# Feed-forward weights of the third stage prepared beside the first and read back beside the second

## The chip, the cores and the metric

The kernel runs on 1 core of one Trainium2 chip. The metric is the device time of one execution in microseconds (us). A core has TensorE (PE; its weight loads are listed as PEld), VectorE (DVE), ScalarE (ACT), GpSimd (POOL) and SyncE (SP), which here only issues DMAs. Each works off its own queue in order, and they wait for each other by semaphores.

## The reference, cut to what matters

The input x has 32 sequences of 64 tokens with 256 features. Six blocks follow one another, each of the form `x = x + block(layernorm(x))`:

```
x = x + attention, 16 heads of 128, causal, with biases
x = x + attention over a given context (no weights)
x = x + _L0_ffn_ref(layernorm(x), ...)          # the third stage
x = x + a scan with cosines and sines of a running sum
x = x + attention over the context, 16 heads of 16
x = x + feed-forward with 4-bit weights, 2048 wide
```

The third, with h and the attention both made from its input z:

```
attn = attention16(rmsnorm(z) * ln1)            # 16 heads of 16, causal
mod  = 0.1 * tanh(attn @ A)                     # A is 256 x 16
h    = rmsnorm(z) * ln2
gate = silu(h @ W_in.T + (mod * (h @ A)) @ B)   # W_in, W_up: 1024 x 256
out  = z + (gate * (h @ W_up.T)) @ W_down.T     # W_down: 256 x 1024
```

## The kernel before

x stays in SBUF as 16 tiles of 128 tokens (`core.x`). Most matrix products are made from pairs of parts: a high part (rounded to fp32r by ScalarE) and a low part (the difference, by GpSimd or VectorE), three products for each. The program is written stage by stage; inside a stage each engine has its own block, and `run_steps` lays out a software pipeline: in step s, part number n with lag L works on unit s - L, in the order of the list. So the place in the list and the lag set an engine's order by hand.

Stage 1 (L340 to about L625) runs over 64 units, 16 heads by 4 groups of tokens; a round is 8 units, two heads. TensorE makes q and k (L440) and, for even heads, v (L422) of a unit, then transposes, scores (L455), the output product (L481) and the product with v (L472) of units further back. Each of these has one PSUM buffer, which ScalarE copies out (L506, L519, L527). The list of ScalarE ends with `split_high` and `deq.scalar`. Beside this `Dequantiser` prepares the last stage's 4-bit weights in 16 pieces: VectorE and ScalarE compute, GpSimd sums (`gpsimd_sum`) and makes the low part (`gpsimd_low`), and SP stores each to DRAM (L2216) in `later_loads`, one step of that per head: the head's weights, then `deq.store`, and in even steps `deq.load` (L2210, two loads). `deq.store` waits for `low_done`, and `gpsimd_low` of a piece stands in GpSimd's queue behind `split_low` and `gpsimd_sum` of later heads.

Stage 2 (L640 to L840) has 32 units. VectorE takes maxima (L721) and subtracts (L725) straight from PSUM.

Stage 3 begins with `token_stats`: `bn_stats` of 16 tiles (L216) unless an earlier stage has gathered them, `bn_aggr` (L219), roots. SP issues all of the stage's loads in this block (L1547 to L1550); the next block starts when every engine is through this one. Then come `split_tokens` (L280, L305), a block that prepares the small weights (among it `m_ps`, L1574), and `attention16` (L1533 on): 16 tiles in a pipeline, for this stage with `beside`, a list of functions for ScalarE and one for GpSimd. ScalarE calls them at odd tiles:

```
def weights(i, rnd, k):
    if i % 2 == 1 and i // 2 < len(beside[0]):
        beside[0][i // 2](act)
```

The list is `in`, `up`, `down` (L1625, the high parts of the feed-forward weights, 128x2048 each) and `high_rows` (L1631, rows of B), which waits for the semaphore `zeroed` to be 2. GpSimd does `residual` for its 16 tiles (L999, L1002) and then `low_parts`: two memsets (L1636) that raise `zeroed`, the three subtracts (L1639), and one for the rows of B (L1644):

```
steps(pool, [(residual if own else rope, 0)])
if beside:
    beside[1](pool)
```

After it `feed_forward` runs, and beside that `EarlyKeys` computes keys for the fifth stage in buffers of the weights (`w["all"]`).

Of the kernel before, what the change touches and what calls it, by code (L numbers as in the profile page):

```python
# [7 lines left out]
STAGES = "12345"  # L8

ALU = mybir.AluOpType  # L10
ACT = mybir.ActivationFunctionType
F32 = mybir.dt.float32
# [4 lines left out]
P = 128  # L17
# [106 lines left out]
class Core:  # L124


    def __init__(self, nc, ctx, ins):
# [8 lines left out]
        self.early_values = nc.dram_tensor("early_values", (P, NT * 2 * 4 * 2 * 17), F32, kind="Internal").ap()  # L136
        self.stored_weights = nc.dram_tensor("stored_weights", (PIECES, P, 6 * D), F32, kind="Internal").ap()
# [174 lines left out]

def stage_L0_attention(core):
# [6 lines left out]
    with ExitStack() as octx:  # L320
# [15 lines left out]
        deq = Dequantiser(core, Room(nc, octx, "s1q"))  # L336

# [19 lines left out]
        def first_loads(sp):  # L357
            sp.dma_start(bo[:, :], ins["L0_attn_b_O"].rearrange("(a n) -> a n", a=1).to_broadcast([P, D])) \
                .then_inc(bo_in, 16)
            load(sp, 0, 0, 0)  # L360
            load(sp, 1, 0, 1)
            deq.load(sp, 0)

        token_stats(core, mv, rstd, "s1n", prefetch=first_loads)
        split_tokens(core, xnT, mv, rstd, "s1t")
        with ExitStack() as ctx:
# [28 lines left out]
            def _(sp):  # L395
                def later_loads(h, rnd, slot):
# [4 lines left out]
                    if slot == 0:  # L401
                        deq.load(sp, rnd)

                run_steps(sp, H, [(later_loads, 0)], unroll=2)
                for j in (PIECES - 2, PIECES - 1):
                    deq.store(sp, j, j % 2)
                for stored in deq.stored:
                    sp.wait_ge(stored, 8 * PIECES)

# [79 lines left out]
            def _(act):  # L489
# [42 lines left out]
                def z_high_part(u, rnd, k):  # L532
# [7 lines left out]
                                   (z_high_part, 4), (split_high, 0), (deq.scalar, 4)], unroll=8)  # L540

            @block.gpsimd
            def _(pool):
                def split_low(h, rnd, slot):
# [3 lines left out]
                    if slot == 0:  # L548
# [3 lines left out]

                run_steps(pool, H, [(split_low, 0), (lambda j, rnd, slot: deq.gpsimd_sum(j), 1),
                                    (lambda j, rnd, slot: deq.gpsimd_low(j, slot), 2)])
# [58 lines left out]
def stage_L0_cross(core):  # L613
# [7 lines left out]
    with ExitStack() as octx:  # L621
# [22 lines left out]
        with ExitStack() as ctx:  # L644
# [26 lines left out]
            @block.sync  # L671
            def _(sp):
                load_context(sp, 1, NT // CHUNK)

# [43 lines left out]
            def _(dve):  # L718
# [21 lines left out]
                run_steps(dve, U, [(shift, 3), (attended, 5)], unroll=2, head=U + 5)  # L740
# [108 lines left out]
def attention16(core, mode, tag, mv, rstd, factor, w, zT=None, mT=None, beside=None, prefetch=None):  # L849
# [6 lines left out]
    with ExitStack() as ctx:  # L856
# [55 lines left out]
        if prefetch:  # L912
# [4 lines left out]
        if own:  # L917
            @block.sync
            def _(sp):
                for i in range(NT):  # L920
# [173 lines left out]

        @block.tensor
        def _(pe):
            pe.wait_ge(masks, 2)
            if not own:
                pe.wait_ge(w["loaded"], 64)
# [273 lines left out]
class EarlyKeys:  # L1373
# [5 lines left out]
    def __init__(self, core, room, w):  # L1379
# [3 lines left out]

        def floats(name):
            return w[name][:, :, :].rearrange("p c n -> p (c n)")
# [5 lines left out]
        self.raw, self.rot = rows(floats("in")[:, 0:n]), rows(floats("in")[:, n:2 * n])  # L1391
        self.spread = w["all"][:, 0:2, :].rearrange("p k n -> p (k n)")
# [7 lines left out]
        self.values = floats("down")[:, 0:2 * n].rearrange("p (t b d) -> p t b d", b=2, d=W)  # L1400
# [106 lines left out]
def stage_L0_ffn(core):  # L1507
    nc, ins = core.nc, core.ins
    F, R = 1024, 16
    with ExitStack() as ctx:  # L1510
# [10 lines left out]
        parts = {n: room.sb(n + "_parts", [P, 2, 2 * F], F32R) for n in ("in", "up", "down")}  # L1521


# [4 lines left out]
        w["all"] = room.sb("all", [P, 3, NC * F])  # L1528
        for n, (name, c) in enumerate((("in", NC), ("up", NC), ("down", F // P))):
            w[name] = w["all"][:, n, :].rearrange("p (c n) -> p c n", c=c)  # L1530
        high_done, low_done, zeroed = room.sems("high_done", "low_done", "zeroed")
        ln = room.sb("ln", [P, 2, NC])
        with ExitStack() as sctx:  # L1533
            sroom = Room(nc, sctx, "s3w")
            for n in ("wq", "wk", "wv", "wo"):
# [6 lines left out]
            loads = (("wq", "WqT"), ("wk", "WkT"), ("wv", "WvT"), ("wo", "L0_ffn_Wo"), ("A", "L0_ffn_A"),  # L1542
                     ("in", "WinT"), ("up", "WupT"), ("down", "WdownT"))

            def load_weights(sp):
                for dst, src in loads:
                    sp.dma_start(w[dst][:, :, :], ins[src].rearrange("(c p) n -> p c n", p=P)).then_inc(w_in, 16)  # L1547
                for at in (0, 32, 64):
                    sp.dma_start(w["B"][at:at + R, :], ins["L0_ffn_B"]).then_inc(w_in, 16)
# [8 lines left out]
            ALL = 16 * (len(loads) + 4)  # L1558
# [41 lines left out]
            def _(dve):  # L1600
# [9 lines left out]
                for n in ("in", "up"):  # L1610
                    for c in range(NC):
                        nc.vector.tensor_scalar(w[n][:, c, :], w[n][:, c, :], ln[:, 1, c:c + 1], None, ALU.mult)
# [10 lines left out]
        def high_part(name):  # L1623
            def part(act):
                nc.scalar.activation(parts[name][:, 0, :], flat(name), ACT.Copy).then_inc(high_done, 1)  # L1625
            return part

        def high_rows(act):
            act.wait_ge(zeroed, 2)
# [4 lines left out]
        def low_parts(pool):  # L1634
            for rows in (b_rows, m_rows):
                nc.gpsimd.memset(rows[:].bitcast(F32), 0.0).then_inc(zeroed, 1)  # L1636
            for n, name in enumerate(parts):
                pool.wait_ge(high_done, n + 1)
                nc.gpsimd.tensor_tensor(parts[name][:, 1, :], flat(name), parts[name][:, 0, :], ALU.subtract) \  # L1639
                    .then_inc(low_done, 1)  # L1640
            pool.wait_ge(high_done, len(parts) + 1)
            pool.wait_ge(low_done, len(parts))
# [3 lines left out]
            pool.wait_ge(low_done, len(parts) + 1)  # L1646

        def flat(name):
            return w[name][:, :, :].rearrange("p c n -> p (c n)")

        def part_of(name):
            return lambda part, c, f: parts[name][:, part, c * F + f * P:c * F + (f + 1) * P]

        attention16(core, "ffn", "s3a", mv, rstd, factor, w, zT, mT, beside=([high_part(n) for n in parts] + [high_rows], low_parts))
        feed_forward(core, "s3f", zT, part_of("in"), part_of("up"),
# [788 lines left out]
```

## Time and profile before

| | |
|---|---|
| median of 3 runs | 1846.08 us (1842.78 to 1849.24) |
| the profiled execution | 1846.89 us, its span 1845.0 us |
| busy in the span | PE 1632.0, PEld 1264.1, DVE 1133.0, ACT 844.6, POOL 684.5 us |
| mean granted clock of TensorE | 0.950 |
| DMA | 67.7 MB, 37 GB/s |

Rows of the view of windows have the stretch and its length, then the busy time (and the number of instructions) of PE, PEld, DVE, ACT and POOL, then the granted clock of TensorE as a share of 2.4 GHz, the busy share of the DMA engines and GB/s. Rows of the timeline have the start, the busy time, the engine, the line of the kernel and the operation with the tiles that it writes and reads; in brackets stands how long the engine was idle before it and what ended that. SPq is the queue of SyncE, where each DMA row is an issue.

### The profile page before, as it was taken

Reading aid. Unit: us, or ns where it says so; the run is one execution under the profiler, and the core shown is the slowest. Engines: PE = TensorE matmul, PEld = TensorE weight load, DVE = VectorE, ACT = ScalarE, POOL = GpSimd, SP = SyncE. Lnnn points to the kernel's source line nnn. Section 1 sums busy time; section 2 is a strip of 40 time slices with the busy share of each in tenths; the row PEclk is TensorE's granted clock in tenths of the full one; section 3 lists DMA queues with packets and bytes.
Section 4 is the critical chain, followed back from the end, with each engine's and each line's share of the span. In section 5 each row is a group of like instructions: output and inputs, shape, how many; then the busy total and the mean of one; then the engine's idle time right before and its main releaser. Section 6 shows DMA issues by size and latency. Waiting matters only on the chain. (4 is left out here: it accounts for less than half of the span.)

```text
span 1845.0 us, 32931 instructions
## 1 busy us (share of the span) xinstructions
PE 1632.0 (88%) x12582; PEld 1264.1 (69%) x12582; DVE 1133.0 (61%) x1852; ACT 844.6 (46%) x1403; POOL 684.5 (37%) x508
## 2 busy tenths in 40 slices
PE   4999999999996886798999778999998598999997
PEld 3888888888884664676887533444444475888886
DVE  6667676776776885765422867998986465111111
ACT  3555455555543663555422335555552474322222
POOL 0021211212123651900422108999995340333332
PEclk9999999999998995999999778999999797999999
DMA  3011111111102003001020100000000900000001
GB/s 99 15 61 58 47 45 57 65 40 60 54 38 87 2 2 96 10 10 45 1 101 0 38 0 0 1 1 0 0 1 1 359 23 1 1 1 1 1 0 45
DMA packets 67247, 67.73 MB, mean 37 GB/s; under 512 B 24208, under 2 KB 60560, under 8 KB 66496
## 3 DMA queue, kind: packets, MB, share of 16 engines
q1 hardware_dynamic: 67136, 66.19, 11.0%
q8 instruction: 77, 1.26, 0.3%
q14 instruction: 34, 0.28, 0.0%
HBM read 45.86 MB, written 19.27 MB: 35 GB/s over the span
## 5 line engine op out<-in xcount | busy, mean ns | idle before, releaser
L546 POOL TENSOR_TENSOR s_w_parts<-s_w_raw,s_w_parts 128x768 fp32r<-128x768 f32 x16 | 29.7, 1853 | 429.3 <-ACT s_w_parts L498 429.3
L1341 DVE TENSOR_TENSOR s6f_hid<-s6f_act_sb,s6f_u_ps 128x512 f32<-128x512 f32 x64 | 44.0, 688 | 218.3 <-PE s6f_u_ps L1292 218.3
L1364 POOL TENSOR_TENSOR s6f_hid_parts<-s6f_hid,s6f_hid_parts 128x512 fp32r<-128x512 f32 x64 | 82.6, 1290 | 226.4 <-ACT s6f_hid_parts L1330 226.4
L2006 POOL TENSOR_TENSOR s4b_pcs<-s4b_cs,s_p_rows 128x1024 f32<-128x1024 f32 x64 | 120.6, 1907 | 95.2 <-ACT s4b_cs L2052 95.2
L2017 POOL TENSOR_TENSOR s4b_with_re<-s4b_with_re,s4b_with_im 128x1024 f32<-128x1024 f32 x64 | 150.6, 2379 | 2.7 <-DVE s4b_with_im L1971 2.7
L2092 PE MATMUL s4b_c_ps<-s4b_pcs,const 128*128 128x512 f32 x256 | 123.3, 605 | 0.0
L422 PE MATMUL s_v_ps<-s_wv_parts,s_xnT 128*128 128x256 f32 x768 | 104.2, 286 | 12.0 <-ACT s_v L527 6.4
L481 PE MATMUL s_o_ps<-s_w_parts,s_zT 128*128 128x256 f32 x768 | 110.3, 294 | 4.2 <-DVE x_rows L585 4.1
L422 PEld LDWEIGHTS s_v_ps<-s_wv_parts,s_xnT 128*128 128x128 f32 x768 | 96.7, 191 | 17.6 <-ACT s_v L527 9.7
L1330 ACT ACTIVATE s6f_hid_parts<-s6f_hid 128x512 fp32r<-128x512 f32 x64 | 40.5, 632 | 144.1 <-PE s6f_o_ps L1312 140.8
L2082 PE MATMUL s4b_turns_ps<-s_theta_bd,s_zc 128*128 128x512 f32 x128 | 77.6, 690 | 31.5 <-DVE s4b_frac L1956 30.4
L1312 PEld LDWEIGHTS s6f_o_ps<-s6w_parts,s6f_hid_parts 128*128 128x128 f32 x768 | 99.2, 188 | 6.8 <-issue 1.0
L481 PEld LDWEIGHTS s_o_ps<-s_w_parts,s_zT 128*128 128x128 f32 x768 | 97.1, 192 | 8.8 <-issue 4.5
L440 PE MATMUL s_q_ps<-s_xnT,s_w_parts 128*128 128x512 f32 x384 | 102.6, 403 | 0.0
L1292 PE MATMUL s6f_g_ps<-s_zT,s6w_parts 128*128 128x512 f32 (+1 forms) x384 | 101.2, 398 | 1.2 <-PEq L260 1.2
L1364 POOL TENSOR_TENSOR s3f_hid_parts<-s3f_hid,s3f_hid_parts 128x512 fp32r<-128x512 f32 x32 | 42.2, 1320 | 161.3 <-ACT s3f_hid_parts L1330 161.3
L1312 PE MATMUL s6f_o_ps<-s6w_parts,s6f_hid_parts 128*128 128x256 f32 x768 | 100.7, 280 | 0.8 <-POOL s6f_hid_parts L1364 0.8
L1292 PE MATMUL s6f_u_ps<-s_zT,s6w_parts 128*128 128x512 f32 (+1 forms) x384 | 100.4, 395 | 0.0
L440 PE MATMUL s_k_ps<-s_xnT,s_w_parts 128*128 128x512 f32 x384 | 98.5, 392 | 0.0
L511 ACT ACTIVATE s_ex<-s_sc 128x256 f32<-128x256 f32 x64 | 26.7, 417 | 144.6 <-DVE s_sc L579 144.6
L2092 PEld LDWEIGHTS s4b_c_ps<-s4b_pcs,const 128*128 128x128 f32 x256 | 49.4, 194 | 60.8 <-issue 58.6
L1292 PEld LDWEIGHTS s6f_u_ps<-s_zT,s6w_parts 128*128 128x128 f32 x384 | 72.2, 188 | 17.9
(310 smaller groups left out, 4006.9 us busy)
## 6 DMA issues: line engine op xcount, KB each, us to landing
stored_weights<-s1q_halves SPq DMA_DIRECT2D x16, 768.0 KB, 3.7
s6w_parts<-stored_weights SPq DMA_DIRECT2D x32, 384.0 KB, 8.0
s1q_packed<-in_codes SPq DMA_DIRECT2D x8, 384.0 KB, 4.4
s1q_scale<-in_scale_rows SPq DMA_DIRECT2D x8, 384.0 KB, 5.0
early_values<-s_vbd SPq DMA_DIRECT2D x1, 2176.0 KB, 12.2
s_vbd<-early_values SPq DMA_DIRECT2D x1, 2176.0 KB, 12.8
x_rows<-in_x SPq DMA_DIRECT2D x1, 2048.0 KB, 8.3
s_w_raw<-in_L_attn_W_Q SPq DMA_DIRECT2D x16, 128.0 KB, 2.2
```

The lines of the kernel that those rows point to most:

```text
L422: last = nc.tensor.matmul(v_ps[:, n * 2 * E:(n + 1) * 2 * E], xnT[:, px, c, g * TG + t, :], wv_parts[:, pw, c, :, :], start=(c == 0 and (p ...
L440: last = nc.tensor.matmul(ps[:, :], weights(slot, pw, m, c), xnT[:, px, c, g * TG:(g + 1) * TG, :], start=(c == 0 and (pw, px) == PARTS[0] ...
L481: last = nc.tensor.matmul(o_ps[:, t // 2, (t % 2) * D:(t % 2 + 1) * D], zT[:, pz, t * P:(t + 1) * P], w_parts[:, k // G, pw, 2, :], start= ...
L1292: last = nc.tensor.matmul(ps[:, s, :], wt(pw, c, f), zT[:, pz, c:c + 1, bass.ds(rnd * TG, TG), :] .rearrange("p c t q -> p (c t) q"), star ...
L1312: last = nc.tensor.matmul(o_ps[:, t, 0:D], hid_parts[:, f % 2, ph, t * P:(t + 1) * P], down_w(pw, f), start=(f == 0 and (ph, pw) == PARTS[0]),
L1330: nc.scalar.activation(hid_parts[:, f % 2, 0, :], hid[:, f % 2, :], ACT.Copy).then_inc(high_done, 1)
L1341: nc.vector.tensor_tensor(hid[:, f % 2, :], act_sb[:, f % 2, :], u_ps[:, f % 2, :], ALU.mult) \
L1364: nc.gpsimd.tensor_tensor(hid_parts[:, f % 2, 1, :], hid[:, f % 2, :], hid_parts[:, f % 2, 0, :], ALU.subtract).then_inc(low_done, 1)
L2006: last = nc.gpsimd.tensor_tensor(pcs[:, half, n_, :].rearrange("p (k c) -> p k c", k=HK), cs[:, half, n_, :].rearrange("p (k c) -> p k c", ...
L2017: nc.gpsimd.tensor_tensor(with_re[:, half, n_, :], with_re[:, half, n_, :], with_im[:, half, n_, :], op).then_inc(sum_done, 1)
L2082: nc.tensor.matmul(turns_ps[:, :], zc[:, half, bass.ds(i * P, P)], theta_bd[:, half, n_ * 64:(n_ + 1) * 64, :].rearrange("p c m -> p (c m) ...
L2092: last = nc.tensor.matmul(c_ps[:, n_, b * 512:(b + 1) * 512], core.c("tri"), pcs[:, half, n_, b * 512:(b + 1) * 512], start=True, stop=True)
```

## The change

- Stage 1 gets a second weight preparation, `FfnWeights`, over 8 pieces of 384 KB (128 partitions, three chunks of 256 numbers: two of gate and up, one of down). In each round SP stores piece r - 1 (768 KB) and loads piece r in the odd steps, behind `deq.store`; ScalarE scales two chunks of it (k = 2) and makes the high part (k = 6), both as the last entry of its list with lag 4; GpSimd makes the low part.
- In stage 2 `StoredFfn` loads the 8 pieces back into SBUF, behind the loads of the context. VectorE gathers `bn_stats` there for each tile once it is final, so that stage 3 need not.
- Stage 3 loses the loads of these weights, their scaling on VectorE (L1612), and the three high parts and three low parts. The rows of B are loaded from `attention16` on. `beside` has only `high_rows` and `low_rows` (the two memsets and the subtract for B's rows). `EarlyKeys` has buffers of its own. Stages 2 and 3 run as one.
- Four matmuls with no use for the result are put in front of the fifth stage's attention, and two per unit in the first four units of the fourth stage's second part.

The core of the diff:

```diff
@@ stage 1: FfnWeights
+    def load(self, sp, rnd):
+        wait(sp, self.low_done, rnd)
+        sp.dma_start(self.raw[:, :, :].unsqueeze(1),
+                     self.ins["ffn_pieces"].rearrange("k p a n -> p k a n")[:, bass.ds(rnd, 1), :, :]) \
+            .then_inc(self.arrived, 16)
+    def store(self, sp, rnd):
+        sp.wait_ge(self.low_done, rnd + 1)
+        sp.dma_start(...).then_inc(self.stored, 16)
+    def scalar(self, u, rnd, k):
+        if k == 2:
+            act.wait_ge(self.ln_in, 16)
+            act.wait_ge(self.arrived, 16 * rnd + 16)
+            for c in range(NC):
+                nc.scalar.activation(self.raw[:, c, :], self.raw[:, c, :], ACT.Identity, scale=self.ln[:, 1, c:c + 1]) \
+                    .then_inc(self.scaled, 1)
+        elif k == 6:
+            act.wait_ge(self.scaled, 2 * rnd + 2)
+            wait(act, self.stored, 16 * rnd)
+            nc.scalar.activation(self.parts[:, 0, :, :], self.raw[:, :, :], ACT.Copy).then_inc(self.high_done, 1)
+    def gpsimd(self, rnd):
+        nc.gpsimd.wait_ge(self.high_done, rnd + 1)
+        nc.gpsimd.tensor_tensor(self.parts[:, 1, :, :], self.raw[:, :, :], self.parts[:, 0, :, :], ALU.subtract) \
+            .then_inc(self.low_done, 1)
@@ stage 1, SP: later_loads
                     deq.store(sp, h - 2, slot)
                     if slot == 0:
                         deq.load(sp, rnd)
+                    else:
+                        ffn.store(sp, rnd - 1)
+                        ffn.load(sp, rnd)
@@ stage 1, lists of ScalarE and GpSimd
-                                   (z_high_part, 4), (split_high, 0), (deq.scalar, 4)], unroll=8)
+                                   (z_high_part, 4), (split_high, 0), (deq.scalar, 4),
+                                (ffn.scalar, 4)], unroll=8)
-                                    (lambda j, rnd, slot: deq.gpsimd_low(j, slot), 2)])
+                                    (lambda j, rnd, slot: deq.gpsimd_low(j, slot), 2),
+                                    (split_ffn, 1)])
@@ stage 2
+                def gather_stats(u, rnd, n):
+                    if u % 2:
+                        dve.wait_ge(added, u + 1)
+                        nc.vector.bn_stats(core.stats[:, u // 2, :], core.x[:, u // 2, :])
-                run_steps(dve, U, [(shift, 3), (attended, 5)], unroll=2, head=U + 5)
+                run_steps(dve, U, [(shift, 3), (attended, 5), (gather_stats, 7)], unroll=2, head=U + 7)
@@ stage 3
         def high_rows(act):
+            act.wait_ge(b_in, 48)
             act.wait_ge(zeroed, 2)
...
-        def low_parts(pool):
+        def low_rows(pool):
             for rows in (b_rows, m_rows):
                 nc.gpsimd.memset(rows[:].bitcast(F32), 0.0).then_inc(zeroed, 1)
-            for n, name in enumerate(parts):
-                pool.wait_ge(high_done, n + 1)
-                nc.gpsimd.tensor_tensor(parts[name][:, 1, :], flat(name), parts[name][:, 0, :], ALU.subtract) \
-                    .then_inc(low_done, 1)
...
-        attention16(..., beside=([high_part(n) for n in parts] + [high_rows], low_parts))
+        attention16(..., beside=([high_rows], low_rows), prefetch=load_rows)
@@ attention16, fifth stage's form only
+        def keep_busy():
+            ident, age = core.c("ident"), core.c("age")
+            for _ in range(4):
+                nc.tensor.matmul(s_ps[:, 0, :], ident, age, start=True, stop=True)
@@ fourth stage, second part
+                def keep_busy(u, i, half):
+                    if isinstance(u, int) and u < 4:
+                        nc.tensor.matmul(o_ps[:, :], core.c("ident"), core.c("age"), start=True, stop=True)
-                run_steps(pe, UNITS, [(phases(0), 0), (running_sums(0), 3), (turn_y, 7), (turn_outs, 6),
-                                      (phases(1), 0), (running_sums(1), 3), (heads, 6), (output, 8)],
+                run_steps(pe, UNITS, [(phases(0), 0), (keep_busy, 0), (running_sums(0), 3), (turn_y, 7), (turn_outs, 6),
+                                      (phases(1), 0), (keep_busy, 0), (running_sums(1), 3), (heads, 6), (output, 8)],
```

## Rows read from the trace of the kernel before

**Rows 1.** The view of windows: stage 1's loop, and the third stage's attention.

```profile
30.00:568.00 538.00, 503.56 (x4096) 449.66 (x4096) 388.33 (x690) 275.44 (x457) 97.85 (x56) 0.99 0.14 48
...
734.00:868.00 134.00, 113.09 (x1600) 93.59 (x1600) 85.44 (x146) 66.41 (x111) 51.07 (x40) 0.95 0.08 10
```

**Rows 2.** The timeline of stage 1: start, length, engine, line, operation [idle before].

```profile
163.35 0.38 SPq L2216 DMA_DIRECT2D stored_weights<-s1q_halves  x1
...
164.44 1.16 SPq L2210 DMA_DIRECT2D s1q_scale<-in_scale_rows  x1
...
166.82 1.64 PE L422 MATMUL s_v_ps<-s_wv_parts,s_xnT 128*128 128x256 f32 x12 [0.92 <-ACT s_v L527]
...
197.32 0.37 SPq L2216 DMA_DIRECT2D stored_weights<-s1q_halves  x1
...
199.57 0.67 ACT L536 ACTIVATE s_zT<-s_z_ps,s_bias 128x512 fp32r<-128x512 f32 x1
...
200.71 0.69 ACT L506 ACTIVATE s_qT<-s_q_ps,s_bias 128x512 f32<-128x512 f32 x1 [0.46 <-PE s_q_ps L440]
...
202.81 0.69 PE L455 MATMUL s_s_ps<-s_kT,s_qT 128*64 128x64 f32 x16 [0.39 <-issue]
```

**Rows 3.** DMA issues from 163 to 172 us: KB each, us from issue to landing.

```profile
s1q_packed<-in_codes SPq DMA_DIRECT2D x1, 384.0 KB, 4.5
s1q_scale<-in_scale_rows SPq DMA_DIRECT2D x1, 384.0 KB, 5.0
```

**Rows 4.** The timeline of TensorE, late in stage 1.

```profile
553.79 0.66 PE L463 MATMUL s_pT_ps<-const,s_prob 128*128 128x128 f32 x4 [2.91 <-DVE s_prob L601]
```

**Rows 5.** The view of windows, 555 to 559 us.

```profile
555.00:559.00 4.00, 3.20 (x16) 3.23 (x17) 2.91 (x6) 0.08 (x1) 0.00 (x0) 0.57 0.00 0
```

**Rows 6.** The view of the tile s1q_sized: duration ns min/median/max.

```profile
L2238 DVE TENSOR_TENSOR s1q_sized<-s1q_over,s1q_code x16: 941/2571/2578, 66.1 to 549.5; 128x768 f32<-128x768 f32 x16
```

**Rows 7.** The timeline, ScalarE and GpSimd, first tiles of the third stage's attention.

```profile
742.06 1.91 ACT L1625 ACTIVATE s_in_parts<-s_all 128x2048 fp32r<-128x2048 f32 x1
...
746.02 0.60 ACT L1035 ACTIVATE s3a_qT<-s3a_qk_ps 128x512 f32<-128x512 f32 x1 [2.06 <-PE s3a_qk_ps L1112]
...
768.84 1.80 POOL L1636 MEMSET s_m_rows<- 80x2048 f32 x1
```

**Rows 8.** The timeline, later tiles of the same.

```profile
769.19 1.23 DVE L950 TENSOR_REDUCE s3a_mx<-s3a_s_ps 128x16 f32<-128x1024 f32 x1 [0.63 <-PE s3a_s_ps L1155]
...
772.84 11.41 DVE L976 SCALAR_TENSOR_TENSOR s_mT<-s_mT,s3a_th 16x128 f32<-16x128 f32 x1
...
785.10 1.01 PE L1213 MATMUL s3a_of_ps<-s3a_attT,s_WoA 128*16 128x128 f32 x4 [8.68 <-issue]
...
793.25 2.11 ACT L1631 ACTIVATE s_b_rows<-s_B 16x1024 fp32r<-16x1024 f32 x2
...
794.15 1.23 DVE L950 TENSOR_REDUCE s3a_mx<-s3a_s_ps 128x16 f32<-128x1024 f32 x1 [0.63 <-PE s3a_s_ps L1155]
...
850.26 1.23 DVE L950 TENSOR_REDUCE s3a_mx<-s3a_s_ps 128x16 f32<-128x1024 f32 x1 [0.64 <-PE s3a_s_ps L1155]
```

**Rows 9.** The timeline, front of the third stage.

```profile
699.37 5.33 DVE L216 BATCH_NORM_STATS2 x_stats<-x_rows 128x6 f32<-128x256 f32 x16 [1.21 <-PEq L168]
...
708.99 0.44 SPq L1550 DMA_DIRECT2D s_ln<-in_ln_ffn  x1
709.88 1.06 DVE L280 TENSOR_SCALAR s3t_xn<-x_rows,s_mv,s_factor 128x256 f32<-128x256 f32 x3 [2.10 <-PEq L189]
```

**Rows 10.** The timeline, VectorE in the second stage.

```profile
635.25 1.23 DVE L721 TENSOR_REDUCE s_mx<-s_s_ps 128x16 f32<-128x1024 f32 x1 [0.74 <-PE s_s_ps L801]
```

**Rows 11.** The timeline of TensorE, twice in the fourth stage and once in the fifth.

```profile
1092.18 2.07 PE L2082 MATMUL s4b_turns_ps<-s_theta_bd,s_zc 128*128 128x512 f32 x2 [1.50 <-DVE s4b_frac L1956]
...
1118.69 1.13 PE L2082 MATMUL s4b_turns_ps<-s_theta_bd,s_zc 128*128 128x512 f32 x2 [0.47 <-DVE s4b_frac L1956]
...
1446.06 0.66 PE L1135 MATMUL s5a_qk_ps<-const,s5a_q_rows 128*128 128x128 f32 x2 [18.39 <-POOL s5a_q_rows L1018]
```

More of the change, by code:

```diff
@@ L362, in first_loads @@
             deq.load(sp, 0)
+            ffn.load_norm(sp)
+            ffn.load(sp, 0)
         token_stats(core, mv, rstd, "s1n", prefetch=first_loads)
@@ L406, in _ @@
                     deq.store(sp, j, j % 2)
+                ffn.store(sp, FFN_PIECES - 1)
                 for stored in deq.stored:
                     sp.wait_ge(stored, 8 * PIECES)
+                sp.wait_ge(ffn.stored, 16 * FFN_PIECES)
             @block.tensor
@@ L910, in values_of @@
             return w["values"][:, i, b, pair // 2, :, :].rearrange("p h e -> p (h e)")
-        if prefetch:
+        if prefetch and not own:
             @block.sync
@@ L1527, in stage_L0_ffn @@
         m_rows = room.sb("m_rows", [64 + R, NT, P], F32R)
[L1528 to L1531, printed above, removed]
+        high_done, low_done, zeroed, b_in = room.sems("high_done", "low_done", "zeroed", "b_in")
         ln = room.sb("ln", [P, 2, NC])
@@ L1620, in _, with load_rows @@
                 nc.vector.tensor_copy(w["WoA"][:, :, :], wa_ps[:, :, 0:R])
[L1623 to L1626, printed above, removed]
+        def load_rows(sp):
+            for at in (0, 32, 64):
+                sp.dma_start(w["B"][at:at + R, :], ins["L0_ffn_B"]).then_inc(b_in, 16)
         def high_rows(act):
+            act.wait_ge(b_in, 48)
             act.wait_ge(zeroed, 2)
@@ L1645, in low_parts, with stage_L0_cross_and_ffn @@
                 .then_inc(low_done, 1)
[L1646 to L1655, printed above, removed]
-                     lambda part, f: parts["down"][:, part, f * D:(f + 1) * D], F, ACT.Silu, (mT, m_rows, b_rows),
-                     stats=True, early=EarlyKeys(core, room, w))
-        core.stats_ready = True
+            pool.wait_ge(low_done, 1)
+        attention16(core, "ffn", "s3a", mv, rstd, factor, w, zT, mT, beside=([high_rows], low_rows), prefetch=load_rows)
+        feed_forward(core, "s3f", zT, stored.gate, stored.up, stored.down, F, ACT.Silu, (mT, m_rows, b_rows),
+                     stats=True, early=EarlyKeys(core, room), ready=stored.ready)
+        core.stats_ready = True
+def stage_L0_cross_and_ffn(core):
+    with ExitStack() as ctx:
+        stored = StoredFfn(core, Room(core.nc, ctx, "s3p"))
+        stage_L0_cross(core, stored.load)
+        stage_L0_ffn(core, stored)
 def stage_L1_attention(core):
```

84 lines of the change are left out of this document (59 added, 25 removed).

## The prediction

> **What bounds the kernel now.** I read the windows first, one per stage, and then the timelines of the engines at the places that the diff touches. In stage 1's loop TensorE is busy for 503.6 of 538 us [rows 1]: its own matmuls set the pace, so whatever makes it wait there lengthens the program. In the third stage's attention it is busy for 113.1 of 134 us [rows 1], and one hole stands out. VectorE's product for `mT`, 16x128 elements, takes 11.41 us, and TensorE then stands idle for 8.68 us [rows 8]. Through that time GpSimd runs the subtracts for the low parts of the feed-forward weights, the first of which starts when the memset that begins at 768.84 us ends [rows 7]. The change takes those subtracts away. Two waits that it puts in matter as much, and for both the question is what the engine that waits has behind it.
>
> **Part 1, stage 1: the piece's load.** The load of piece r is issued on SP in step h = 2r+1, behind two stores. The older of these, `deq.store`, waits for GpSimd and is issued at 197.32 us in round 2 [rows 2]. ScalarE asks for the piece in `ffn.scalar` at k = 2 with lag 4, step 8r+6, right after the `zT` copy of unit 8r+2. That copy starts at 199.57 and ends at 200.24 us [rows 2]: only 2.9 us after the store's issue. Before, in the even steps, SP issues one store of 768 KB and two loads of 384 KB. The second load goes out 1.09 us after the store and lands 5.0 us later [rows 2, 3], so 1,536 KB have landed 6.1 us after the store's issue. The new trio is two stores and one load, 1,920 KB. With time in proportion to bytes it lands after 7.6 us. If only the load's own latency counts (issue at +1.1, then 4.5 as in [rows 3]) it is 5.6 us. I take 6.8, nearer to the bytes, since all of it was asked for at once in both cases.
>
> ScalarE then scales two chunks of 256 elements (about 0.85 us, estimated from 0.69 us for 512 [rows 2]) and only then copies q and k for the next unit. In round 2 the copy of q would start at 197.32 + 6.8 + 0.85 = 204.97 us instead of 200.71 [rows 2]; the two copies back to back take 1.3, so TensorE's scores start at 206.3 instead of 202.81: 3.5 us late (2.3 and 4.3 by the bounds). Its queue is in order, and behind the scores stand the output and `weigh`, so nothing covers this. Rounds 1 to 7 pay, round 0 was loaded early: 7 x 3.5 = +24.5 us (16 to 30).
>
> The clock: TensorE would be idle for about 3.9 us. Late in stage 1 it was idle for 2.91 us [rows 4], and in the 4 us from 555 the granted clock is 0.57 [rows 5], so 3.4 of them at 1.2 GHz, 1.7 us of work lost. I take 1.65 per round, 7 x 1.65 = +11.6 us (0 to twice that).
>
> **Part 2, the other additions to stage 1.** The high part, one activation of 128x768, goes between the `zT` copy and the copy of v in step 8r+10. There TensorE already waits for ScalarE (0.92 us at 166.82 [rows 2]), so about 0.8 us, estimated as above, is paid in full: 8 x 0.8 = +6.4 us (0 to 7). The low part is 768 columns on GpSimd, after its other work of the round. The rows show what that can do: a VectorE sum that takes 941 ns alone has a median of 2571 [rows 6], 1.63 us more, while GpSimd works. Behind the new subtract I find VectorE on operations with PSUM operands, and take 0; the bound is 8 x 1.63 = 13. The Trainium skill (SBUF — State Buffer, "Who interferes with whom") says that a VectorE instruction with two SBUF inputs contends with a GpSimd one that reads SBUF, and that the later one blocks for the whole instruction. By it up to one subtract is paid per round, the same upper bound; and by it the product of [rows 8] should have waited for one subtract, where it waited for three in a row. At the end of stage 1 the last piece's store lies behind the last `deq.store`: +0.3 us (0 to 2).
>
> **Part 3, second stage and the front of the third.** `bn_stats` of 0.33 us each (5.33 for 16 [rows 9]) go to VectorE just ahead of a gap of 0.74 us [rows 10], where it waits for scores: hidden, and 0.45 us at the very end. Without that gap it would be 16 x 0.4 = 6.4. In front of the third stage the statistics no longer stand before `bn_aggr`, and SP no longer issues eleven loads before `ln`, which holds the block open till 709.43 us, VectorE's next start being 709.88 [rows 9]. With five loads of 0.5 us both end some 7 us sooner: -6.8 us net, with 0.3 for a stage boundary less (bounds -4 and -7.5). The 6 MB read back are asked for in the second stage and used some 170 us later: nothing. The four scalings of 128x1024 and the smaller loads lie beside TensorE's `m_ps`: nothing.
>
> **Part 4, the third stage's attention.** `beside[0]` had four entries, called at tiles 1, 3, 5 and 7; `high_rows` was the fourth, at 793.25 us [rows 8]. Now it is the only one, so it comes at tile 1, where `in_parts` was, at 742.06 [rows 7]. It waits for `zeroed` 2, and the memsets that raise it stand in GpSimd's queue behind all 16 tiles of `residual`: the second ends at 768.84 + 1.80 = 770.6 us [rows 7]. Until then ScalarE can't do the first exponent, and TensorE has only scores and projections of two tiles. Then `high_rows` itself takes 3.1 us (2.11 for two of its three activations [rows 8]), so ScalarE's copy of q for tile 2 starts at 773.7, not 746.02 [rows 7]: +27.7 us (24 to 28). TensorE restarts at 1.2 GHz: +2.4 (0 to 4). Against this the hole goes. Two tiles from 769.19 to 794.15 took 24.96 us; the eight from 794.15 to 850.26 took 7.01 each [rows 8], so the hole cost 24.96 - 14.02 = 10.9 us (late clock and `high_rows` included). Gone too is ScalarE's work in tiles 1, 3 and 5, 1.91 us each, mostly hidden: -1.2 (0 to -4).
>
> **Part 5, matmuls to keep TensorE busy.** In the fourth stage a step takes 2.07 us of matmul and then 1.50 of idle time [rows 11]; at 2.4 GHz the same matmul takes 1.13. Seven steps could gain 0.94 each, the first two lose 0.5 where a matmul of 2.07 is put in a gap of 1.50: I take -4 us (+1 to -6). In the fifth, four of them fit in the idle 18.39 us [rows 11] and the next tiles start at a higher clock: -2 (0 to -4).
>
> **Sum.** 24.5 + 11.6 + 6.4 + 0.3 - 6.8 + 27.7 + 2.4 - 10.9 - 1.2 - 4 - 2 = +48.0 us. The profiled execution took 1846.9 us (span 1845.0), 0.8 above the median 1846.1, so about 1894 us.
>
> **The rivals.**
> (a) The piece is there in time, or its wait costs TensorE nothing and leaves its clock: 1894 - 24.5 - 11.6 = 1858 us. It needs a landing within 2.9 us of the store's issue, against 5.0 for one load alone [rows 3], or slack, against 94% busy.
> (b) The holds are dearer: the clock stays low twice as long (+11.6) and GpSimd's subtract hits a VectorE operation each time (+13): 1919 us. For it speaks [rows 6], against it the operands of what runs there.
> (c) The other side, faster: TensorE has enough work ahead in both places to cover ScalarE's holds. All of 24.5 + 11.6 + 6.4 + 27.7 + 2.4 = 72.6 us would be gone: 1821 us; the kernel is faster once 66% of it is covered. Against it: in [rows 8] it had under 3 us of work when VectorE was held.
> (d) The change does not do what it says (the subtracts' stall moves elsewhere whole, the front gains nothing, holds half covered): about 1846.
>
> **The numbers.** The sum 60%, (a) 14%, (b) 13%, (c) 10%, (d) 3%. The sum's own bounds are 1876 to 1911 us; the range goes out to (a) and (b): 1856 to 1922. About 0.3% is what a measurement of this kernel can tell from no change; faster by more 10%, within 3%, slower 87%.
>
> **What would show it.** In stage 1, once per round from round 1, ScalarE idle for about 4 us until the piece has landed, and TensorE idle and then at 0.5 of its clock; rounds longer by some 6 us, from the second on. In the third stage, ScalarE idle from tile 1 for 28 us until a GpSimd memset, then `high_rows`; no VectorE instruction of 11 us. The next block's VectorE start some 3.6 us into the third stage. The prediction is wrong if the piece's wait is short or round-free, if TensorE works through the hold at tile 1, or if the matmuls put in for the clock give much more than 6 us.

## The result, and the profile after

The changed kernel took 1906.68 us (median of 4 runs, 1903.88 to 1909.09) beside 1847.66 us for the kernel before (4 runs): ratio 1.0325, 95% interval 1.0305 to 1.0345, slower by 59 us. The forecast was 1894 us with a range of 1856 to 1922. The profiled execution took 1904.54 us, its span 1902.8.

The forecast was +48.0 us; the spans differ by 57.8 and the medians by 59.0. To see where the 57.8 us arose, I took the start of the first or last instruction of one kind at each seam. The distance between two seams is what the stage between them took, and the column "added" says by how much the change lengthened it.

| seam | before | after | added since the seam above | forecast |
|---|---|---|---|---|
| stage 1, last sum into x | 565.4 | 611.9 | +46.5 | +42.5 |
| stage 2, first maximum | 578.5 | 627.1 | +2.1 | +0.3 |
| stage 2, last `s_att` | 697.9 | 744.4 | -2.1 | 0 |
| stage 3, last copy of zT | 720.9 | 760.4 | -7.0 | -6.8 |
| attention, first maximum | 743.7 | 782.9 | -0.3 | 0 |
| attention, last maximum | 856.4 | 913.9 | +18.3 | +18.0 |
| feed-forward, last gate | 1005.0 | 1064.9 | +2.4 | 0 |
| fourth stage, second part, first `frac` | 1091.4 | 1153.9 | +2.6 | 0 |
| its last `frac` | 1377.7 | 1437.9 | -2.3 | -4 |
| fifth stage, last maximum | 1532.9 | 1589.6 | -3.5 | -2 |
| end of the span | 1845.0 | 1902.8 | +1.1 | 0 |

(42.5 is 24.5 + 11.6 + 6.4; 18.0 is 27.7 + 2.4 - 10.9 - 1.2.) One profiled execution stands on each side, and a stage without any edit can differ by 2 us between two of them (last section).

**Stage 1.** The windows of the third and of a later loop round in the changed kernel, then the timeline of the third round's step (SP, ScalarE, TensorE) and of the same place a round later, TensorE's waits from 60 to 620 us, and what the piece's tile says of all rounds:

```profile
205.05:276.57 71.52, 63.85 (x514) 57.17 (x514) 47.01 (x83) 35.63 (x60) 13.97 (x8) 0.98 0.19 65
347.32:419.05 71.73, 64.82 (x514) 58.16 (x514) 47.00 (x83) 35.64 (x60) 13.96 (x8) 0.95 0.19 64
```

```profile
205.05 0.37 SPq L2308 DMA_DIRECT2D stored_weights<-s1q_halves  x1
205.62 0.35 SPq L342 DMA_DIRECT2D ffn_weights<-s1f_parts  x1
206.06 1.95 SPq L335 DMA_DIRECT2D s1f_raw<-in_ffn_pieces  x1
...
212.80 0.91 ACT L352 ACTIVATE s1f_raw<-s1f_raw,s1f_ln 128x256 f32<-128x256 f32 x2 [4.82 <-DMA s1f_raw<-in_ffn_pieces]
213.61 0.67 ACT L593 ACTIVATE s_qT<-s_q_ps,s_bias 128x512 f32<-128x512 f32 x1
...
214.95 0.94 PE L542 MATMUL s_s_ps<-s_kT,s_qT 128*64 128x64 f32 x16 [4.76 <-ACT s_qT L593]
...
245.91 1.68 PE L509 MATMUL s_v_ps<-s_wv_parts,s_xnT 128*128 128x256 f32 x12 [1.64 <-ACT s_v L614]
...
276.57 0.37 SPq L2308 DMA_DIRECT2D stored_weights<-s1q_halves  x1
...
277.58 1.05 SPq L335 DMA_DIRECT2D s1f_raw<-in_ffn_pieces  x1
...
283.53 0.91 ACT L352 ACTIVATE s1f_raw<-s1f_raw,s1f_ln 128x256 f32<-128x256 f32 x2 [4.02 <-DMA s1f_raw<-in_ffn_pieces]
```

```profile
PE s_s_ps L542 <- ACT s_qT L593: 28.5, 7, 4.8
```

```profile
  DMA s1f_raw<-in_ffn_pieces: 28.9, 7
...
DMA to landing us min/median/max: 5.2/5.9/6.7
```

The chain is the one that was worked out. In the round shown the three transfers go out at 205.05, 205.62 and 206.06; ScalarE stands 4.82 us until the third has landed, and TensorE 4.76 us until ScalarE has copied q (in the six other rounds about 4.0). ScalarE waits 28.9 us in 7 times, 4.1 each. From the first store's issue to the landing it is 7.75 us here, where the issue of the load took SP 1.95 us, and 7.0 in the six others (205.05 to 212.80; 276.57 to 283.53). In the view of DMA over this stretch the engines are 80 to 100% busy in most slices from 205.8 to 211 us: the load shares them with 1,536 KB of stores. [rows 2] have the same scores with 0.39 us of idle time, and the product with v with 0.92. VectorE is busy for 47.0 us of a round, as against 46.8 before: GpSimd's new subtract hits nothing there.

**The third stage's attention.** The timeline of ScalarE, GpSimd and TensorE at tile 1 of the changed kernel:

```profile
780.09 1.27 ACT L1142 ACTIVATE s3a_kbd<-s3a_qk_ps,const 128x512 f32<-128x512 f32 x2 [2.05 <-PE s3a_qk_ps L1219]
809.75 2.12 ACT L1724 ACTIVATE s_b_rows<-s_B 16x1024 fp32r<-16x1024 f32 x2 [28.39 <-POOL s_m_rows L1729]
811.88 1.05 ACT L1724 ACTIVATE s_b_high<-s_B 16x1024 fp32r<-16x1024 f32 x1
812.96 0.60 ACT L1136 ACTIVATE s3a_qT<-s3a_qk_ps 128x512 f32<-128x512 f32 x1
...
807.85 1.80 POOL L1729 MEMSET s_m_rows<- 80x2048 f32 x1
...
815.98 1.12 PE L1274 MATMUL s3a_pT_ps<-const,s3a_ex 128*128 128x128 f32 x4 [29.07 <-ACT s3a_ex L1162]
```

ScalarE stands 28.39 us until the memset of 807.85 us has ended, which stands behind all of `residual`; then come the 3.2 us of `high_rows`. TensorE is idle for 29.07 us and comes back at half clock (1.12 us for a group of four that took 0.66 in [rows 4]). The hole of [rows 8] is gone: the product for `mT` takes 269 to 281 ns in all 16 tiles.

**The front of the third stage**, timeline of VectorE and SP:

```profile
744.36 0.29 DVE L829 TENSOR_TENSOR s_att<-s_o_ps,s_rs 128x128 f32<-128x128 f32 x1
...
745.22 0.43 DVE L837 BATCH_NORM_STATS2 x_stats<-x_rows 128x6 f32<-128x256 f32 x1 [0.23 <-POOL x_rows L806]
745.95 1.17 DVE L220 BATCH_NORM_AGGREGATE s_mv<-x_stats 128x2 f32<-128x6 f32 x16 [0.30 <-PEq L737]
...
748.37 0.47 SPq L1646 DMA_DIRECT2D s_ln<-in_ln_ffn  x1
```

The next block starts on VectorE at 749.38 us, 3.4 us after `bn_aggr`; in [rows 9] the statistics alone took 5.33 us and SP issued until 709.43.

### The profile page after: what moved, and what is told of

Read it like the earlier page. It is cut to its first block and busy times, and to the rows that moved or that the text cites. A ratio compares the mean times of both kernels' runs of the same rounds, so it can differ in the third digit from the quotient of the medians.

```text
span 1902.8 us, 33049 instructions
## 1 busy us (share of the span) xinstructions
PE 1654.2 (87%) x12606; PEld 1282.8 (67%) x12606; DVE 1119.7 (59%) x1848; ACT 850.9 (45%) x1424; POOL 685.7 (36%) x513
## 5 line engine op out<-in xcount | busy, mean ns | idle before, releaser
L568 PE MATMUL s_o_ps<-s_w_parts,s_zT 128*128 128x256 f32 x768 | 118.2, 307 | 4.0 <-DVE x_rows L678 4.0
L568 PEld LDWEIGHTS s_o_ps<-s_w_parts,s_zT 128*128 128x128 f32 x768 | 104.2, 205 | 9.1 <-issue 4.6
L2174 PE MATMUL s4b_turns_ps<-s_theta_bd,s_zc 128*128 128x512 f32 x128 | 73.5, 657 | 27.6 <-DVE s4b_frac L2044 26.5
L2184 PEld LDWEIGHTS s4b_c_ps<-s4b_pcs,const 128*128 128x128 f32 x256 | 48.8, 192 | 60.1 <-issue 57.8
```

Of the source, the lines that this page charges most:

```text
L568: last = nc.tensor.matmul(o_ps[:, t // 2, (t % 2) * D:(t % 2 + 1) * D], zT[:, pz, t * P:(t + 1) * P], w_parts[:, k // G, pw, 2, :], start= ...
L2174: nc.tensor.matmul(turns_ps[:, :], zc[:, half, bass.ds(i * P, P)], theta_bd[:, half, n_ * 64:(n_ + 1) * 64, :].rearrange("p c m -> p (c m) ...
L2184: last = nc.tensor.matmul(c_ps[:, n_, b * 512:(b + 1) * 512], core.c("tri"), pcs[:, half, n_, b * 512:(b + 1) * 512], start=True, stop=True)
```

## The experiments

Each was timed against the kernel before on the same chip; "changed" is the kernel after the change, 1906.7 us. The ratio compares all runs of both kernels; the distance between two medians can differ from it by 3 us.

| kernel | median us (runs) | ratio to before, 95% interval |
|---|---|---|
| a: changed, `high_rows` at tile 7 | 1876.65 (4) | 1.0154 (1.0110 to 1.0198) |
| b: changed, memsets first | 1874.78 (4) | 1.0141 (1.0099 to 1.0184) |
| c: changed, piece's load first | 1862.19 (6) | 1.0068 (1.0039 to 1.0097) |
| d: changed, piece asked for later | 1866.77 (4) | 1.0104 (1.0062 to 1.0146) |
| e: b and c | 1831.17 (5) | 0.9902 (0.9869 to 0.9934) |
| f: e, high part at k = 2 | 1854.34 (12) | 1.0036 (1.0016 to 1.0056) |
| g: f, no matmuls without use | 1858.27 (12) | 1.0048 (1.0026 to 1.0070) |
| h: f, statistics in stage 3 | 1860.61 (8) | 1.0057 (1.0031 to 1.0083) |
| i: before, six half subtracts | 1846.64 (1) | no interval |
| j: before, a wait between subtracts | 1838.72 (10) | 0.9952 (0.9927 to 0.9978) |
| k: e, high part at k = 3 | 1829.06 (6) | 0.9893 (0.9856 to 0.9931) |
| l: before, with the matmuls without use | 1845.63 (12) | 0.9970 (0.9946 to 0.9994) |

**a and b: ScalarE's hold at tile 1.**

```diff
# a
-        attention16(..., beside=([high_rows], low_rows), ...)
+        attention16(..., beside=([lambda act: None] * 3 + [high_rows], low_rows), ...)
# b: on GpSimd
+            if beside:
+                beside[2](pool)            # the two memsets
             steps(pool, [(residual if own else rope, 0)])
             if beside:
+                pool.wait_ge(y_done, 2 * NT)
                 beside[1](pool)
```

> high_rows is called at tile 7 of the third stage's attention, as before the change, instead of at tile 1; nothing else differs from the changed kernel. My theory: ScalarE's idle time of tile 1 (until GpSimd's second memset) goes whole, because by tile 7 the memsets are done. The third stage's attention, from its first to its last maximum, took 112.7 us before and 131.0 in the changed kernel; it should take 131.0 - 27.7 - 2.4 = 101 us (98 to 104), and the whole some 30 us less: 1877 us. First rival, the work of high_rows itself and not its wait is what costs: then TensorE still waits some 3 us at tile 7 and the attention takes about 104 to 106. Second rival, the hole that the subtracts left before comes back with the one small subtract, 16x1024, that is left: VectorE waits 2.3 us at tile 8, and not 11.

> high_rows stays at tile 1, but GpSimd does its two memsets (2.75 us together) ahead of its 16 tiles of residual and not behind them. My theory: what ScalarE waited for was the place of the memsets in GpSimd's queue, so the same 30 us come back as with high_rows at tile 7, less up to 3 us for its three activations in the pipeline's filling: 1877 to 1881 us. Rival, the cost was tile 1 itself (a pipeline that is just filling has no work ahead, the rows of B are not there yet): then ScalarE still waits at tile 1 for the load of B or TensorE for ScalarE, and over 8 us stay.

They gave 30.0 and 31.9 us. The attention, first to last maximum, went from 131.0 to 103.3 us in both, 27.7 us; another 2.3 us lie in the feed-forward behind it (see what is said of +2.4 us below). In b `high_rows` runs at tile 1, and TensorE waits there for 1.34 us instead of 29.07 (ScalarE, then TensorE):

```profile
781.67 1.27 ACT L1145 ACTIVATE s3a_kbd<-s3a_qk_ps,const 128x512 f32<-128x512 f32 x2 [2.00 <-PE s3a_qk_ps L1222]
782.82 2.11 ACT L1727 ACTIVATE s_b_rows<-s_B 16x1024 fp32r<-16x1024 f32 x2
...
789.81 0.81 PE L1277 MATMUL s3a_pT_ps<-const,s3a_ex 128*128 128x128 f32 x4 [1.34 <-ACT s3a_ex L1165]
```

So neither tile 1 nor the work of `high_rows` was the cost, but the place of the memsets in GpSimd's queue. In a the small subtract that is left lengthens the product for `mT` from 0.28 to 1.10 us, once.

**c and d: the piece's load in stage 1.**

```diff
# c: later_loads, on SP
                     load(sp, h, rnd, slot)
+                    if slot == 1:
+                        ffn.load(sp, rnd)
                     deq.store(sp, h - 2, slot)
...
                         ffn.store(sp, rnd - 1)
-                        ffn.load(sp, rnd)
# d: FfnWeights.scalar
-        if k == 2:
+        if k == 4:
```

> In stage 1 the load of the piece is issued ahead of both stores of its step instead of behind them; ScalarE asks for it at the same place. My theory: ScalarE's wait (28.9 us in 7 times) goes to zero, because the load goes out some 15 us sooner; TensorE gets back 3.6 us of idle time and 1.6 us of low clock per round, 7 x 5.2 = 36 us: 1870 us, rounds of 66.2 us instead of 71.35 (before the change 64.9). What stays is the high part, 0.7 us per round, and 0.6 us that I have not placed. Rival, the three transfers together are too slow and not the place of the load in the queue: then the store that is now last delays what waits for it, and under 20 us come back. Second rival, the clock drops anyway late in the program: only 25 us come back.

> In stage 1 ScalarE scales the piece at k = 4 instead of k = 2, two units (16 us) later; the queue of SP is as in the changed kernel. My theory: the same as with the load first, 1870 us and rounds of 66.2 us, since the piece lands 7.8 us after the step's first store and is now asked for 18 us after it. The two scalings (1.0 us) lie at another unit; if that one has no slack, up to 7 x 0.7 = 5 us less come back than with the load first. Rival as there: under 20 us come back if the transfers themselves and not the wait cost TensorE its time.

c gave 44.5 us and d 39.9, both more than expected. The window of a loop round of c:

```profile
199.47:265.03 65.56, 62.26 (x515) 55.66 (x514) 46.91 (x83) 35.60 (x60) 13.98 (x8) 1.00 0.21 70
```

TensorE is busy for 62.26 us where it was 63.85 to 64.82 with the wait: the low clock costs 1.6 us in the first loop rounds and 2.6 in the later ones, in which it fell for longer. The rest is idle time: 3.6 us in most rounds, 4.4 in one (4.76 - 0.39). Over the seven rounds TensorE's waits of 28.5 us, less the 0.39 that stand there anyway, are 25.8 us. A round of c is 0.66 us longer than before the change, and that is the high part (1.64 - 0.92 = 0.72 us). In d ScalarE's scalings at k = 4 still cost TensorE 0.9 us in each round (its wait for q is 1.3 where 0.4 is usual), while in c the same scalings at k = 2 cost nothing; hence 5 us less.

**e: both places mended.**

> The changed kernel with two places undone: the piece's load ahead of both stores of its step (it gave 44.5 us by itself) and GpSimd's memsets ahead of residual (31.9 us by itself). My theory: the two lie in different stages and have nothing to do with each other, so the gains add up: 1906.7 - 44.5 - 31.9 = 1830 us (1826 to 1834), which is faster than before the change by 0.9%. Rival, both gains have a common part (the clock of later stages, which also moved in the single runs by 1 to 2 us per stage): then the sum is short by 3 to 6 us, 1833 to 1836.

The sum holds: 1831.2 us, 75.5 below the changed kernel and about 1% below the kernel before. Without the two holds nothing of the loss is left.

**f and k: the high part elsewhere.** It is TensorE's last known cost in stage 1.

```diff
# f: no wait for k == 6, right behind the scalings at k == 2
-        elif k == 6:
# k
-        elif k == 6:
+        elif k == 3:
```

> As the one before, and in stage 1 the high part of the piece is made at k = 2, right behind the two scalings, instead of at k = 6. My theory: at k = 6 each 0.83 us is paid (TensorE waits for the copy of v, 1.64 us instead of 0.92); at k = 2 ScalarE has room, as in the step two units later, where two activations of 1.86 us together cost TensorE 0.1. So 0.6 to 0.7 us per round come back, 8 rounds: 5 us, 1825 us, rounds of 64.9 to 65.1 us instead of 65.56. Rival, the room at k = 2 is used up by the scalings (ScalarE waits only 0.44 us for k there): then at least half of the 0.83 us is paid again, rounds of 65.3 to 65.6, 1828 to 1830 us.

> As the kernel with both places undone (1831.2 us), but the high part of the piece at k = 3 instead of k = 6. At k = 2 it was a loss: there ScalarE waited for the store of the piece before, which is issued behind the step's first store and lands 4.6 us later, 11.6 us in 7 times. My theory: at k = 3 that store landed 4 us before (issued at 199.9, landed at 204.5, ScalarE there at 208.7), and the step has room for one more activation of 0.83 us, so 0.6 us per round come back: rounds of 64.9 to 65.1 us instead of 65.56, 1826 us. Rival, the room is not there: ScalarE waits 0.69 us for k in that step and 0.14 to 0.83 us are paid; rounds of 65.2 to 65.6 and 1829 to 1831 us.

f missed badly: 23 us slower than e, and in the profiles stage 1 ends 21.5 us later (571.1 and 592.6). The timeline of SP, ScalarE and TensorE in f:

```profile
203.40 0.35 SPq L342 DMA_DIRECT2D ffn_weights<-s1f_parts  x1
...
209.17 0.84 ACT L356 ACTIVATE s1f_parts<-s1f_raw 128x768 fp32r<-128x768 f32 x1 [2.60 <-DMA ffn_weights<-s1f_parts]
...
211.27 1.12 PE L542 MATMUL s_s_ps<-s_kT,s_qT 128*64 128x64 f32 x16 [3.29 <-ACT s_qT L593]
```

The high part overwrites the buffer that the store of the piece before still reads. ScalarE waits for that store 11.6 us in 7 times, and TensorE for `s_qT` 16.4 us in 7 times. I had looked for room on ScalarE and not for this wait: the same trap as in the change, a transfer issued behind `deq.store` and asked for at once.

k has no such wait and no idle time at k = 3 (0.39 us before the scores, as usual), yet its rounds are 65.58 us, as e's. The gain was lost at another engine. VectorE, GpSimd and ScalarE in k:

```profile
229.17 2.56 POOL L362 TENSOR_TENSOR s1f_parts<-s1f_raw,s1f_parts 128x768 fp32r<-128x768 f32 x1
230.85 1.17 DVE L673 TENSOR_TENSOR s_sc<-s_sc,s_mx 128x256 f32<-128x256 f32 x1
232.05 0.42 ACT L599 ACTIVATE s_ex<-s_sc 128x256 f32<-128x256 f32 x1 [7.06 <-DVE s_sc L673]
```

With its high part ready early, GpSimd's subtract no longer waits for it (3.90 us in e) but runs on at once behind its other work, and there stands over VectorE's `s_sc` with two SBUF inputs: 1.17 us instead of 0.42, and the exponent 0.75 us later. The high part's place cost 0.72, so the two cancel. In e the subtract comes later (at 233.86) and meets nothing: `s_sc` takes 0.42. The 2 us between the medians of e and k are within their spread.

**h: the statistics.** It undoes `gather_stats` in f.

> As the best so far (with the matmuls), but the statistics of the third stage are taken in one row at its front, as before the change, and not in the second stage; its loads stay the fewer. My theory: VectorE's 16 bn_stats, 5.33 us, come back in front of bn_aggr and nothing hides them, less some 0.6 us for the last statistics and the wait for GpSimd's last sum that stand at the second stage's end now: 4.7 us more, 1830 us. Rival, the loads alone had held the front (before the change, SP issued until 709.43 us): then hardly anything changes, since the loads are still few, and the gain was theirs.

It is 6.3 us slower than f in the medians; in the profiles the stretch from the last `s_att` to the last copy of zT went from 16.0 to 20.9 us, +4.9, as expected. The timeline has the 5.33 us of statistics back in a row:

```profile
728.21 5.33 DVE L217 BATCH_NORM_STATS2 x_stats<-x_rows 128x6 f32<-128x256 f32 x16 [0.88 <-PEq L737]
```

Before the change that stretch took 23.0 us. What h keeps of the gain, 2.1 us, is mostly the wait for SP: from `bn_aggr` to the next block's start it is 5.15 us in [rows 9] and 3.37 in h (733.57 to 736.94).

**g and l: the matmuls without use.**

> As the one before, without the matmuls that have no use for their result: the four ahead of the fifth stage's attention and the sixteen in the fourth stage's second part. My theory: they are worth what the profiles of before and after differ in there: 2.3 us in the fourth stage's second part and 2.4 to 3.5 us from its end to the end of the fifth stage's attention, so 5 to 6 us more without them: 1830 us. Rival, what the profiles show is the clock's own coming and going and not these matmuls: then the time stays within 2 us.

> The kernel before the change with the twenty matmuls without use alone: four ahead of the fifth stage's attention and two per unit in the first four units of the fourth stage's second part. The prediction gave them 6 us, the profiles of before and after some 5, and leaving them out of the mended kernel cost 3.9 us, of which its profile shows only 1 to 2.4 us in the stages where they stand. My theory now: they are worth 2 to 4 us, 1843 us. Rival, they are worth nothing and the clock's own coming and going made the differences: within 1 us of before.

Leaving them out of f costs 3.9 us between the medians and 2.2 by the ratios (1.0048 and 1.0036, whose intervals overlap). Adding them alone to the kernel before gains 2.5 us between the medians and 5.5 by the ratio (0.9970, interval 1 to 10 us). By the profiles of f and g, 1.0 us lies in the fourth stage's second part (285.2 and 286.2) and 0.6 behind it; the fifth stage up to its last maximum took 155.1 us in both. Another 4 us had come up in the stages ahead, which have the same instructions. All profiles together say more, ten with the matmuls and four without (before, g, i, j): the fourth stage's second part took 283.5 to 285.3 us with them, 284.7 in the mean, and 286.0 to 286.3 without; the fifth, to its last maximum, 151.2 to 155.1, 152.7 in the mean, and 154.9 to 155.2. That makes 1.5 and 2.3 us, and l beside i and j, where nothing else differs in these stages, has 0.8 and 2.2.

**i and j: the hole of the kernel before.**

```diff
# i: each subtract in two of 1024 columns
# j
                 nc.gpsimd.tensor_tensor(parts[name][:, 1, :], flat(name), parts[name][:, 0, :], ALU.subtract) \
                     .then_inc(low_done, 1)
+                pool.wait_ge(low_done, n + 1)
```

> The kernel before the change, each of the three subtracts cut into two of 1024 columns without a wait between them (six back to back). It tells whether VectorE gets in at the end of an instruction of GpSimd. If it does, its product takes under 3 us; if the hold lasts from one instruction to the next while GpSimd has work issued, it is again 11 us. My theory, from the 11.41 us that spanned the ends of two subtracts, is 11 us and no change in time (1846 us).

> The kernel before the change, with one thing more: GpSimd waits for each of its three subtracts of 2048 columns to end before it issues the next. My theory: VectorE's product took 11.41 us because the three subtracts (4.6, 4.5 and 4.5 us) followed one another without a gap and it could not get in between; with a gap it gets in after the first, so it takes 2 to 4 us, the hole of TensorE (8.68 us) shrinks to about 1 us, and the whole gains 6 to 9 us: 1839 us. First rival, VectorE waits for all of GpSimd's subtracts whatever lies between: no change, 1846 us. Second rival, it gets in but is then held again by the second and the third at its next operations, which have no PSUM operand or two SBUF inputs: the gain is under 3 us.

j gave 9.4 us between the medians (8.9 by the ratio) for a wait on GpSimd, and in its profile the attention took 101.8 us instead of 112.7. GpSimd's subtracts in the kernel before, beside the product that ran from 772.84 to 784.25 us [rows 8], then the product in i and in j:

```profile
770.61 4.58 POOL L1639 TENSOR_TENSOR s_in_parts<-s_all,s_in_parts 128x2048 fp32r<-128x2048 f32 x1
775.14 4.51 POOL L1639 TENSOR_TENSOR s_up_parts<-s_all,s_up_parts 128x2048 fp32r<-128x2048 f32 x1
779.60 4.50 POOL L1639 TENSOR_TENSOR s_down_parts<-s_all,s_down_parts 128x2048 fp32r<-128x2048 f32 x1
```

```profile
771.99 9.52 DVE L976 SCALAR_TENSOR_TENSOR s_mT<-s_mT,s3a_th 16x128 f32<-16x128 f32 x1
...
779.03 4.68 POOL L1640 TENSOR_TENSOR s_down_parts<-s_all,s_down_parts 128x1024 fp32r<-128x1024 f32 x2
```

```profile
770.94 4.58 POOL L1639 TENSOR_TENSOR s_in_parts<-s_all,s_in_parts 128x2048 fp32r<-128x2048 f32 x1
773.12 2.54 DVE L976 SCALAR_TENSOR_TENSOR s_mT<-s_mT,s3a_th 16x128 f32<-16x128 f32 x1
775.59 4.57 POOL L1639 TENSOR_TENSOR s_up_parts<-s_all,s_up_parts 128x2048 fp32r<-128x2048 f32 x1
```

Without waits VectorE did not get in at the ends of four half subtracts; it ended at 781.5 us, near the end of the fifth. That one came before the last, so it doesn't wait until GpSimd has run out of subtracts; what let it in there no run shows. With a wait it ended at 775.66, when the first subtract did.

## Why the prediction was right, step by step

- **Part 1, the piece's wait.** Right in mechanism, place and rounds, and undersized. It was put at 24.5 + 11.6 = 36.1 us; c took 41.1 us out of stage 1's end (611.9 to 570.8). The idle time was nearly right, 24.5 forecast and 25.8 measured: the landing was taken at 6.8 us from the store's issue and was 7.0 in six rounds. Only the round shown, with 7.75, came to the 7.6 that time in proportion to bytes gave. ScalarE's scalings, added on top with 0.85, stand in the chain as taken (q's copy starts 0.81 us after the landing); they cost nothing only where the wait is gone, as in c. The term that was mis-sized is the clock: 1.65 us per round or 11.6 were taken, and of the 41.1 us 15.3 are left beside the idle time; TensorE's busy time shows 1.6 us of it in an earlier round and up to 2.6 in the later ones. Why it stayed low for longer in the later rounds no run shows.
- **Part 2.** The high part: 0.8 forecast, 0.72 waited, 0.66 per round in c. GpSimd's subtract: 0, as taken; k shows that the bound was real, 0.75 us where the subtract moves by 4 us. The end of stage 1: +0.3 forecast, +2.1 measured; the last store goes out at 610.90 us and lands 4.8 us later, and the next block starts at 616.95, after VectorE was idle for 2.39 us, where it was 0.70 before. I took this wait to be hidden behind the one for `deq.store`. No run takes the store away.
- **Part 3.** -6.8 forecast, -7.0 measured; h shows 4.9 of it to be the statistics, and in its profile most of the other 2.1 lies where SP issued the loads. No run undid the loads alone.
- **Part 4.** The mechanism is right, and the hold and the end of the hole together are +18.3 where +18.0 was forecast. That it is so close is partly luck, for two errors cancel. In the attention a and b bring back 27.7 us, where 30.1 was forecast for the hold and the clock after it. What they leave is 9.4 us below the kernel before (103.3 and 112.7), where 10.9 + 1.2 was forecast. j alone has 10.9 for the hole, so the 1.2 for ScalarE's activations is not seen; but the attention takes 101.7 to 104.7 us in kernels without hold and hole (a, b, e, f, g, h, j, k), so differences below 3 us are not decided here.
- **Part 5.** The 5.8 us between the seams are one profile on each side. Over all profiles the fifth stage has 2.3 us where 2 were forecast, and the fourth 1.5 where 4 were. That term was oversized although the matmul takes 1.12 us from the third step on instead of 2.07, as worked out. In two of the steps TensorE then waits for VectorE instead:

```profile
1158.22 1.12 PE L2174 MATMUL s4b_turns_ps<-s_theta_bd,s_zc 128*128 128x512 f32 x2 [0.30 <-DVE s4b_frac L2044]
...
1164.74 1.13 PE L2174 MATMUL s4b_turns_ps<-s_theta_bd,s_zc 128*128 128x512 f32 x2 [1.91 <-DVE s4b_frac L2044]
```

- **The range.** The sum's own bounds, 1876 to 1911 us, are narrower than the bounds of its terms added up, some 1854 to 1939; the prediction doesn't say how it came from the one to the other. The measured time lies inside both.
- **The rivals.** (a), that the piece's wait costs nothing, falls by c. (b), dearer holds, at 1919 us is as near in time as the sum; in mechanism it is half right: the low clock did cost more in stage 1, by some 3.7 us (15.3 for 11.6) and not by 11.6, and the subtract did not. (c), cover, falls by a and b: ScalarE's 28.39 us of idle time came out as 29.07 at TensorE. The work that it had in [rows 8] was 3.6 us (its last group there ended at 776.42 us, the product had begun at 772.84), and not under 3, as the prediction says. (d) falls with the front.
- **The two stages that had no forecast.** +2.4 and +2.6 us appear in the feed-forward's beginning and the fourth stage's first part. Neither is the change's. For the feed-forward (before 148.6, after 151.0), c and d have 148.8 with the hold at tile 1 as it was, and a and b 148.7 without it: the 151.0 is that one execution, at a mean granted clock of 0.97 where c had 0.99 and the kernel before 1.00. The fourth stage's first part took 86.4 us in the profile of before, but 88.5, 88.2 and 88.3 in i, j and l, which have its instructions unchanged, and 89.0 after; its granted clock was 0.82 before, 0.78 in i, j and l and 0.79 after. The same holds, the other way, for the -2.1 of stage 2 (119.4 before; 117.3, 117.2 and 117.3 in i, j and l; 117.3 after). So these three show no effect of the change, only how far the clock moves a stage from one execution to another.

## What to carry to other kernels

When a transfer is added to a queue, work out from the trace what stands ahead of it and when the data is asked for. Here, the order of two lines on SP decided 44 us, and the place of two memsets on GpSimd some 30. A function in a list by position changes its time when entries before it go: look at what it waits for at its new place. And when work is moved into a gap of one engine, check its buffers' readers and what its consumer will then run beside; both of my own moves of the high part came to nothing, f by a store that still read the buffer, k by what GpSimd's subtract then ran beside.

## What the runs showed of the hardware

- **GpSimd holds VectorE beyond one instruction.** VectorE's product (16x128, two SBUF inputs) waited through subtracts that followed one another, 11.41 us in [rows 8] and 9.52 us with six shorter ones; with a semaphore wait between them it took 2.54, and 0.28 with nothing beside it. The Trainium skill (SBUF — State Buffer, "Who interferes with whom") says that whoever issues first gets the shared pair of ports for the whole instruction and the other blocks. By that i would have shown about 2.3 us at most, an estimate from the 4.72 us that two half subtracts took. The measurement decides: while GpSimd has its next instruction ready, VectorE can wait several out.
- **The clock moves unchanged stages by 2 us.** At the end of stage 2 the same matmuls ran at a granted clock of 0.53 before, near the lower level of 1.2 GHz, and at 1.00 after. The windows of the two, before first:

```profile
691.50:697.50 6.00, 5.83 (x72) 5.03 (x72) 0.62 (x3) 2.35 (x4) 0.91 (x2) 0.53 0.00 0
```

```profile
740.00:746.00 6.00, 3.58 (x72) 3.07 (x72) 2.44 (x9) 2.56 (x5) 1.36 (x3) 1.00 0.00 0
```

That is where the -2.1 us of stage 2 in the table come from, with 72 matmuls in each. A difference of 2 us in one stage of one profile says nothing of an edit; e, with a profiled execution of 1836.3 us beside a median of 1831.2, would have misled by 5.
